# Feed-forward features spilled in their own layout, silu ahead of the high half, and the output's residual sum on GpSimd

## The reference, cut to what matters

```python
x = x + layernorm(attention(layernorm(x)))      # attention over channels, 512 x 512 scores
x = x + layernorm(ffn(layernorm(x)))

def ffn(h):                                      # h: 4096 tokens x 512
    gate_w, up_w, down_w = splines(gate_cp), splines(up_cp), splines(down_cp)   # 2048x512, 2048x512, 512x2048
    inter = silu(h @ gate_w.T) * (h @ up_w.T)
    return inter @ down_w.T
```

## Time and profile before

| | us |
|---|---|
| median of 3 runs | 811.36 (811.29 to 813.33) |
| the profiled execution, its own time | 814.72 |
| its span, first to last instruction | 812.9 |
| TensorE busy | 692.6 (85%) |
| VectorE busy | 533.7 (66%) |
| GpSimd busy | 441.7 (54%) |
| ScalarE busy | 374.3 (46%) |
| mean granted clock of TensorE, as a share of the full one | 0.929 |

### The profile page before, as it was taken

How to read it: one execution, slowest core, us unless ns; L and a number is a source line. 1 busy time by engine, 2 the same in 40 slices (tenths; PEclk the granted TensorE clock), 3 DMA queues, 4 the chain that set the end, 5 groups by cost and what they waited for, 6 DMA issues and landing times. The chain is left out here.

```text
span 812.9 us, 16523 instructions
## 1 busy us (share of the span) xinstructions
PE 692.6 (85%) x5872; PEld 482.2 (59%) x5872; DVE 533.7 (66%) x993; ACT 374.3 (46%) x635; POOL 441.7 (54%) x615
## 2 busy tenths in 40 slices
PE   6997899999999999997466987969879698794996
PEld 3765668787778878676123654635546455452555
DVE  7676763696369636746475867959669497672553
ACT  3432233333233323333465755747557476573651
POOL 5199768185928598014254653636536365362542
PEclk9898999999999999999587998989989899897899
DMA  7615556145714474018826153463543635426223
GB/s 242 257 52 180 184 187 216 49 163 178 241 55 148 161 254 132 13 53 228 268 71 169 62 154 112 123 177 113 152 116 113 178 112 137 117 80 164 78 66 104
DMA packets 60687, 115.01 MB, mean 141 GB/s; under 512 B 12880, under 2 KB 25296, under 8 KB 58576
## 3 DMA queue, kind: packets, MB, share of 16 engines
q1 hardware_dynamic: 60624, 114.16, 45.9%
HBM read 81.76 MB, written 32.37 MB: 140 GB/s over the span
## 5 line engine op out<-in xcount | busy, mean ns | idle before, releaser
L1331 POOL TENSOR_TENSOR act<-inter,act 128x512 f16<-128x512 f32 x128 | 158.4, 1245 | 141.2 <-ACT act L1372 141.2
L1445 DVE SCALAR_TENSOR_TENSOR inter<-ubank,c_up,gated 128x512 f32<-128x512 f32 x128 | 95.5, 746 | 62.6 <-ACT gated L1376 61.8
L1586 PE MATMUL ybank<-down,act 128*128 128x160 f16 x512 | 115.4, 243 | 0.0
L1376 ACT ACTIVATE gated<-gbank,c_gate 128x512 f32<-128x512 f32 x128 | 87.7, 685 | 59.9 <-PE gbank L1545 58.2
L1587 PE MATMUL ybank<-down,act 128*128 128x160 f16 x512 | 114.6, 242 | 0.0
L1588 PE MATMUL ybank<-down,act 128*128 128x160 f16 x512 | 114.2, 241 | 0.0
L1372 ACT CAST act<-inter 128x512 f16<-128x512 f32 x128 | 79.2, 619 | 73.1 <-DVE inter L1445 71.6
L1545 PE MATMUL gbank<-z,s_all 128*32 128x512 f16 x512 | 54.7, 418 | 45.4 <-DMA z<-token_features 28.7
L1545 PE MATMUL ubank<-z,s_all 128*32 128x512 f16 x512 | 55.3, 422 | 29.8 <-DVE inter L1445 29.4
L1586 PEld LDWEIGHTS ybank<-down,act 128*128 128x128 f16 x512 | 52.0, 102 | 40.0 <-issue 36.8
L1476 DVE SCALAR_TENSOR_TENSOR x_res<-y,orr,x_res 128x512 f32<-128x512 f32 x32 | 39.2, 1225 | 52.4 <-DMA x_res<-x 44.4
(11 more groups left out here) (195 smaller groups left out, 1972.0 us busy)
## 6 DMA issues: line engine op xcount, KB each, us to landing
x_ln<-x SPq DMA_DIRECT2D x64, 256.0 KB, 3.3
job<-job_in SPq DMA_DIRECT2D x24, 640.0 KB, 4.6
z<-token_features SPq DMA_DIRECT2D x16, 768.0 KB, 5.7
shared<-x SPq DMA_DIRECT2D x32, 256.0 KB, 2.7
x<-shared SPq DMA_DIRECT2D x32, 256.0 KB, 2.0
token_features<-z_hi SPq DMA_DIRECT2D x128, 64.0 KB
x_res<-x SPq DMA_DIRECT2D x32, 256.0 KB, 2.7
out<-x_res SPq DMA_DIRECT2D x32, 256.0 KB, 2.1
```

The costliest lines, as they stand in the source:

```text
L1331: pool.tensor_tensor(hidden[par][:, i, TOK:2 * TOK], inter[:, i % INTERS, :], hidden[par][:, i, 0:TOK], ALU.subtract).then_inc(inter_ready, 1)
L1376: act.activation(gated[:, slot % 2, :], gbank[:], ACT.Silu, scale=c_gate[:]).then_inc(silu_done, 1)
L1445: dve.scalar_tensor_tensor(out=inter[:, i % INTERS, :], in0=ubank[:], scalar=c_up[:], in1=gated[:, i % 2, :], op0=ALU.mult, op1=ALU.mult). ...
L1586: pe.matmul(out, hidden[par][:, r, high], box[:, 0], start=False, stop=False)
```

## The change

1. `spill` writes z to DRAM as it lies in SBUF, 64 rows of 4 x 512 values in one DMA per part (high powers, picked columns, low powers), so three per half instead of twelve; the DRAM tensor is (3, 128, 4, 512) instead of (3, 4, 8, tiles, 512). `load_z` does the reordering: four DMAs per half of 32 partitions each, (f, k) along the partitions, pieces of 512 values (1 KB) in DRAM, instead of two with 4096 values in one run. The host orders coefficients and points to match.
2. `regroup` spills both halves and then loads both, and the reload after tile 0 stands ahead of it.
3. On ScalarE `silu_at(n + 2)` stands ahead of `high(n + 1)` in each step.
4. `o_finish` moves from VectorE to GpSimd, as a plain sum; the mean goes in as the bias of `o_norm`, for which GpSimd makes its negative with one more small subtract. `o_norm` waits for that (`o_mr`) instead of for `o_rstd`.
5. TensorE's groups 2 to 5 are written out instead of looped.

```diff
     def spill(self, sp, half, g, buf=0):
+        K, high, low = self.K, self.z_parts[buf][0], self.z_parts[buf][1]
         rows = slice(half * P // 2, (half + 1) * P // 2)
-        for n in range(first, self.SPILLS if last is None else last):
-            if half == 0 and n == 0:
-                sp.wait_ge(self.z_hi_done, (g + 1) * self.Q * 2)
-            if half == 0 and n == 2 * K:
-                sp.wait_ge(self.z_ready, (g + 1) * self.Q)
-            part, k = (1, 2, 0)[n // K], n % K
-            source = (low[rows, k, :], high[rows, k, :], high[rows, K + k, :])[part]
-            dest = self.spilled[part, k][:, half * tiles:(half + 1) * tiles, :]
-            sp.dma_start(dest.rearrange("f t n -> t f n"), source).then_inc(self.z_spilled[half], 16)
+        if half == 0:
+            sp.wait_ge(self.z_hi_done, (g + 1) * self.Q * 2)
+        sp.dma_start(self.spilled[1, rows], high[rows, 0:K, :]).then_inc(self.z_spilled[half], 16)
+        sp.dma_start(self.spilled[2, rows], high[rows, K:2 * K, :]).then_inc(self.z_spilled[half], 16)
+        if half == 0:
+            sp.wait_ge(self.z_ready, (g + 1) * self.Q)
+        sp.dma_start(self.spilled[0, rows], low[rows, 0:K, :]).then_inc(self.z_spilled[half], 16)
...
     def load_z(self, sp, feats, g, par, half):
...
-        sp.dma_start(z[0:rows, tiles, :], feats.spilled[:, :, :, tiles].rearrange("a k f t n -> (a k f) t n")
-                     ).then_inc(self.z_loaded[par][half], 16)
-        sp.dma_start(z[rows:P, tiles, :], feats.spilled[1, :, :, tiles].rearrange("k f t n -> (k f) t n")
-                     ).then_inc(self.z_loaded[par][half], 16)
+        for at, part in enumerate((0, 1, 2, 1)):
+            source = feats.spilled[part, half * P // 2:(half + 1) * P // 2]
+            sp.dma_start(z[at * group:(at + 1) * group, tiles, :],
+                         source.rearrange("(t f) k n -> (f k) t n", f=POWERS)).then_inc(self.z_loaded[par][half], 16)
...
# regroup
                 for half in range(2):
-                    sp.wait_ge(z_loaded[1 - par][half], loads_before * 32)
-                feats.spill(sp, 0, g, buf=1 - par)
-                feats.spill(sp, 1, g, 0, feats.SPILLS // 2, buf=1 - par)
-                ffn_in.load_z(sp, feats, g, par, 0)
-                feats.spill(sp, 1, g, feats.SPILLS // 2, buf=1 - par)
-                ffn_in.load_z(sp, feats, g, par, 1)
+                    sp.wait_ge(z_loaded[1 - par][half], loads_before * 64)
+                    feats.spill(sp, half, g, 1 - par)
+                for half in range(2):
+                    ffn_in.load_z(sp, feats, g, par, half)
...
# SyncE's quad
                     for before, q in outputs(g, i, 2):
                         finish(before, q)
-                        if j != 1:
-                            reload(before, q)
-                if j == 1:
-                    if not (isinstance(g, int) and g == GROUPS - 1):
-                        regroup(g + 1, 1 - par, count)
-                    for before, q in outputs(g, 6, 2):
                         reload(before, q)
+                if j == 1 and not (isinstance(g, int) and g == GROUPS - 1):
+                    regroup(g + 1, 1 - par, count)
...
# GpSimd
-                pool.tensor_tensor(orr[:, q, 2:3], omv[:, q, 0:1], orr[:, q, 1:2], ALU.mult).then_inc(o_mr, 1)
+                pool.tensor_tensor(orr[:, q, 2:3], omv[:, q, 0:1], orr[:, q, 1:2], ALU.mult).then_inc(o_neg, 1)
+                pool.wait_ge(o_neg, n)
+                pool.tensor_tensor(orr[:, q, 2:3], o_zero[:], orr[:, q, 2:3], ALU.subtract).then_inc(o_mr, 1)
+
+            def o_finish(g, q):
+                n = held(pool, g * Q + q + 1)
+                pool.wait_ge(res2_loaded[q], held(pool, g * 16 + 16))
+                pool.wait_ge(o_normed, n)
+                pool.tensor_tensor(x_res[:, q % 2, :], y[:, q % 2, :], x_res[:, q % 2, :], ALU.add).then_inc(out_ready, 1)
...
+                    for before, q in outputs(g, i, 2):
+                        o_finish(before, q)
                     if s == 1 and begun:
                         feats.scale(pool, g * Q + j + AHEAD + 1)
...
# ScalarE
-                act.wait_ge(o_rstd, held(act, g * Q + q + 1))
-                act.activation(y[:, q % 2, :], y[:, q % 2, :], ACT.Copy, scale=orr[:, q, 1:2]).then_inc(o_normed, 1)
+                act.wait_ge(o_mr, held(act, g * Q + q + 1))
+                act.activation(y[:, q % 2, :], y[:, q % 2, :], ACT.Identity, scale=orr[:, q, 1:2],
+                               bias=orr[:, q, 2:3]).then_inc(o_normed, 1)
...
+                    if not last:
+                        silu_at(n + 2, (s + 2) % 4)
                     if not (last and n == STEPS - 1):
                         if i + 1 < I:
                             high(g, n + 1, i + 1, par)
                         else:
                             high(g + 1, n + 1, 0, 1 - par)
-                    if not last:
-                        silu_at(n + 2, (s + 2) % 4)
...
# VectorE: o_finish and its calls are gone
-                dve.scalar_tensor_tensor(out=x_res[:, q % 2, :], in0=y[:, q % 2, :], scalar=orr[:, q, 2:3],
-                                         in1=x_res[:, q % 2, :], op0=ALU.subtract, op1=ALU.add).then_inc(out_ready, 1)
...
# TensorE
-            schedule(pe, quad)
+            schedule(pe, quad, loop=False)
```

More of the change, by code:

```diff
@@ L304, in body @@
                         feats.load(sp, x1_t, XR + t, t)
-                    if not more and t < 2:
-                        feats.spill(sp, 1, 0, t * SPILLS // 2, (t + 1) * SPILLS // 2)
+                    if not more and t == 0:
+                        feats.spill(sp, 1, 0)
                     if not more and t == 4:
@@ L988, in load, with spill @@
         sp.dma_start(self.x_ln[:, slot, :], x1_t[m]).then_inc(self.ln_loaded[slot], 16)
-    def spill(self, sp, half, g, first=0, last=None, buf=0):
-        K, tiles = self.K, self.spilled.shape[3] // 2
-        high, low = self.z_parts[buf]
+    def spill(self, sp, half, g, buf=0):
+        K, high, low = self.K, self.z_parts[buf][0], self.z_parts[buf][1]
         rows = slice(half * P // 2, (half + 1) * P // 2)
-        for n in range(first, self.SPILLS if last is None else last):
-            if half == 0 and n == 0:
-                sp.wait_ge(self.z_hi_done, (g + 1) * self.Q * 2)
-            if half == 0 and n == 2 * K:
-                sp.wait_ge(self.z_ready, (g + 1) * self.Q)
-            part, k = (1, 2, 0)[n // K], n % K
-            source = (low[rows, k, :], high[rows, k, :], high[rows, K + k, :])[part]
-            dest = self.spilled[part, k][:, half * tiles:(half + 1) * tiles, :]
-            sp.dma_start(dest.rearrange("f t n -> t f n"), source).then_inc(self.z_spilled[half], 16)
+        if half == 0:
[5 more added lines that the diff above has]
+        sp.dma_start(self.spilled[0, rows], low[rows, 0:K, :]).then_inc(self.z_spilled[half], 16)
     def constants(self, pool):
@@ L1235, in ffn_block, with schedule @@
         block = ctx.enter_context(nc.Block())
-        def schedule(engine, quad):
+        def schedule(engine, quad, loop=True):
             def group(g, par, count, made, begun, more):
@@ L1245, in schedule @@
             group(1, 1, 1, Q, Q, True)
-            with engine.Fori(0, GROUPS // 2 - 2) as pair:
-                for par in range(2):
-                    group(2 * pair + (2 + par), par, pair + 2, Q, Q, True)
+            if loop:
+                with engine.Fori(0, GROUPS // 2 - 2) as pair:
+                    for par in range(2):
+                        group(2 * pair + (2 + par), par, pair + 2, Q, Q, True)
+            else:
+                for g in range(2, GROUPS - 2):
+                    group(g, g % 2, g // 2 + 1, Q, Q, True)
             group(GROUPS - 2, 0, GROUPS // 2, 2, 1, False)
@@ L1351, in quad @@
                         o_scale(before, q)
+                    for before, q in outputs(g, i, 2):
+                        o_finish(before, q)
                     if s == 1 and begun:
                         feats.scale(pool, g * Q + j + AHEAD + 1)
+            pool.memset(o_zero[:], 0.0).then_inc(o_cleared, 1)
+            pool.wait_ge(o_cleared, 1)
             pool.sem_inc(part_done, 2 * PARTS)
@@ L1362, in _ @@
             o_scale(GROUPS - 2, Q - 1)
+            o_finish(GROUPS - 2, Q - 1)
             for q in range(Q):
                 o_scale(GROUPS - 1, q)
+                if q:
+                    o_finish(GROUPS - 1, q - 1)
+            o_finish(GROUPS - 1, Q - 1)
         @block.scalar
@@ L1521, in _ @@
             o_stats(GROUPS - 2, Q - 1)
-            o_finish(GROUPS - 2, Q - 1)
             for q in range(Q):
@@ L1874, in feature_tables @@
     features = np.stack([high, low, pick.astype(np.float16)], 1)
+    coef, near = coef.transpose(1, 0, 2, 3), near.transpose(1, 0, 2, 3)
     coef = np.concatenate([coef.reshape(K * POWERS, 5, -1), near.reshape(K * WINDOW, 5, -1)])
```

(4 more changed lines are left out.)

22 lines of the change are left out of this document (7 added, 15 removed).

## The result

The changed kernel takes 767.78 us (median of 4 runs, 767.4 to 770.52) against 811.33 (810.61 to 813.33): ratio 0.9467, 95% interval 0.9439 to 0.9495, faster. The forecast was 747 us in a range of 731 to 770, so the time lies inside the range but 20.8 us above the figure, close to rival A's 772. The profiled execution took 767.43 us, its span 765.6. The profiled execution before took 814.72 us, 3.4 above its median, so the spans differ by 47.3 us and the medians by 43.6: 3.7 us of a gain that is read from these spans and carried over to the median, as the forecast does, are not there.

A forecast was written before the change was run, and what follows sets the result against it. TensorE was taken as busiest, its idle time from late z and x_res loads. Gains of 48.3 (five groups), 5.6, 4.1 and 7.8, less 1.1 for the tail, made 64.7: 811.36 to 747 us, range 731 to 770.

The forecast's parts named there:

- rival A: Groups 1 to 6: z comes as late as before if pieces move near 195 GB/s; 25.2 us, 772 us; chance 0.20.
- VectorE's wait for x_res: VectorE waits 44.4 us in six places for x_res; claimed gone, the tile 2 load being issued some 18 us sooner.
- the jump's wait: TensorE's loop jump, one 5.4 us wait, hidden behind the x_res wait; writing groups out holds the gain, adds none.
- rival C: ScalarE's norm, now Identity, makes it reload its table: 82 us; if all exposed, 829 us, slower; chance 0.04.
- rival B: GpSimd becomes the bound: 28 quads each run 1.0 us over the cover, 28 us in all, 775 us; chance 0.08.
- The tail: Last 7.10 us of the kernel: 1.1 longer, 0.54 ahead of the norm and 1.27 - 0.75 for the sum.
- the prediction's own signs: Profile signs: z waits 0 to 2 us and 41 to 42 us groups if right; z waits of 3 or more mean rival A.
- The undisturbed group, 40.4 us: Full group's sixteen steps without a stall, nearly all matmul: 40.4 us, from four steps taking about 10.1.
- The start of the spills, 2.7 us later: SyncE's first spill moves from 566.34 to 569.0, behind GpSimd's later sum, the tile 0 store and the x_res reload.
- From the first spill to z, 11.9 us: Regrouping chain from its start until z has landed: 11.9 us at 263 GB/s, where before it was 18.1.
- The residual stall: TensorE's remaining z wait in the five groups: 1.0 us instead of 4.1 in four, 2.7 instead of 6.4 in one.
- Group 1: Group 1's gain: 4.1 - 1.0 us of z stall plus 1.0 of clock, 4.1 us.

The follow-up runs named there:

- 128 rows: Changed kernel with each half's z loads as four DMAs to all 128 partitions instead of 32, two 1 KB pieces each, features scrambled: 755.32 us, ratio 0.9257.
- half 0 first: Changed kernel with only SyncE's order changed: spill half 0, reload x_res, load half 0, then spill and load half 1: 741.23 us, ratio 0.9081.

## Why the prediction was right, and where its number was not

*Right in kind.* VectorE's wait for x_res goes, product is on time, the jump's wait goes, no table is loaded (rival C falls), and GpSimd is no bound (rival B falls: without z's chain the groups are 40.2 to 40.5 us). The tail is 7.10 us in both, where the forecast had it 1.1 longer. By the prediction's own signs, z waits of 3 us and groups 44.7 apart, rival A came true in part.

*The undisturbed group, 40.4 us.* Right to 0.2 where z is on time, but by luck in part: it is 10.7 for the first four steps and 9.9 for each other four, where the forecast had 10.1 four times. And silu, costed at nothing in full groups, is worth 1.0 of it, by the traces since it keeps GpSimd's `low` out of VectorE's way.

*The start of the spills, 2.7 us later.* Right: 1.8 for the reload (2.8 us from store to first spill instead of 1.0) and 0.9 for the sum.

*From the first spill to z, 11.9 us: the step that failed.* It took 14.6. The rate of 263 GB/s was scaled up from a stretch at a DMA share of 0.41; at full share the 64-row spills and 32-row loads move at about 215. The issue of the six spills, 0.42 us each, was too small as well (5.7 us in all), but it hides under their bytes (7.3 us at 215). Against rival A the forecast counted the issue of all 24 old spills, 12 us, as won; only 18 of them stood ahead of the first z load, 10.9 us. z came 3.1 us late, where the forecast kept 1.0 and rival A had 4.1, so rival A had the mechanism. The Trainium skill's figure for few rows (SBUF — State Buffer, "Door 1: The DMA port swizzle"), which the forecast weighed, put z 2 us late; the trace agrees with its rate in the main, about 215 against about 218 GB/s.

*The residual stall.* Forecast 4 x 1.0 + 2.7 = 6.7 us in the five groups, measured 17.1; the slow clock behind the stalls, which the sum left out there, covers the other 2.8 missing in them: the first steps after the stalls that end at 476.02, 520.69, 565.35, 609.76 and 655.01 take 4.4, 4.2, 4.1, 5.3 and 2.8 us, where 3.25 is usual without a stall, and the clock in their first 2 us is 0.50 (1.2 GHz), after 2.6 to 3.3 us of idle time, in all but the last (1.00, after 2.6). Group 1 was forecast 4.1 us better and is 0.2: its clock is 0.89 where it was 0.96.

*What the sum did not see.* The chain's order is the better remedy than its rate (741.2 us against 755.3 with 128 rows): the 786 KB that nobody waits for yet stood ahead of the 1049 KB that TensorE waits for. The forecast even lists them in that order. Reordered, the same transfers at the same rate give 741.2 us, 3.5% below the changed kernel.

## What to carry to other kernels

When one queue carries both what is needed next and what is needed later, sum the bytes ahead of the first before asking for a better layout. Where the data of the next group starts from a point in this group, that chain is the period: an edit that sends its first link out later costs in every group, even if it relieves an engine. A rate scaled up from a half-busy stretch is at best an upper bound, and a transfer to fewer partitions needs a row of its own kind.

## What the runs showed of the hardware that was not expected

- Loads in 1 KB pieces moved at 305 to 322 GB/s into 128 partitions and at 203 to 242 into 32, 8 KB pieces into 32 partitions at 208 to 246, all at a share of 0.88 or more.
- A spill of 256 KB was issued in 0.47 us on an idle queue and, in the changed kernel, in 1.1 to 1.2 behind three others that had not landed. Behind four z loads just issued it took 0.46 (half 0 first), so the bytes under way alone do not set it; what does is not shown.
- ScalarE's norm with a bias from SBUF took 0.81 us against 0.72 without, and no table load.
- The residual sum of 128x512 took 1.27 us on GpSimd every time, and 0.75 to 1.69 on VectorE, the long ones beside GpSimd. VectorE's `norm` of the same shape took 0.54 us alone and 0.74 to 1.43 beside GpSimd's `low`.
